# A language-model tower on one core: the prologue between two attention stages becomes 41 small items placed between the parts of attention units

## The reference

```python
h = tok(x)                       # 3 hashed n-gram embeddings per token, concatenated, @ proj_w
h = h + attn(layernorm(h))       # three softmax attentions over the 1024 tokens
h = h + ffn(layernorm(h))        # 32 experts, each takes its 256 best tokens

# attn, per sequence x (1024 x 128):
x_down = conv1d(x, dw, stride=2) + db                     # 512 x 128
a = softmax(q(x) k(x_down)^T * scale);  out_cross = ln(a v(x_down))   # keys: 512
a = softmax(q(x) k(x)^T * scale);       out_dot   = ln(a v(x))        # keys: 1024
a = softmax(qn(x) kn(x)^T / t);         out_cos   = ln(a v(x))        # q, k of unit length
gate = softmax([out_cross, out_dot, out_cos] gw^T + gb)
z = gate0 * out_cross + gate1 * out_dot + gate2 * out_cos
```

## Time and profile before

| | |
|---|---|
| Median of three runs | 1472.56 us |
| The profiled execution | 1471.54 us, its span 1469.3 us |
| PE busy | 1192.1 us (81%) |
| DVE, ACT, POOL busy | 806.1, 641.0, 838.0 us |
| Start of the first unit's maximum | 94.10 us |
| Start of the last unit's maximum | 1079.75 us |
| Start of the second part | 1110.83 us |

### The profile page before, as it was taken

The page is one execution under the profiler, slowest core; times in us unless marked ns, Lnnn a source line. Parts: engine busy times, 40 slices in busy tenths (PEclk is TensorE's granted clock), DMA queues, the critical chain, the costliest instruction groups (busy, mean ns, idle before and its releaser), DMA issues. The chain is left out here.

```text
span 1469.3 us, 25145 instructions
## 1 busy us (share of the span) xinstructions
PE 1192.1 (81%) x7567; PEld 1042.5 (71%) x7567; DVE 806.1 (55%) x2470; ACT 641.0 (44%) x1578; POOL 838.0 (57%) x1223
## 2 busy tenths in 40 slices
PE   3689989998999999799989989998973334666673
PEld 2469968986997898699879969977963323555553
DVE  4256674666667466556656755666775676211110
ACT  0245545554554555356545545654533424211110
POOL 5344764776476467737666764762470002588785
PEclk9889999999999999899999999999985555888786
DMA  2000001001100100100010001001001000344442
GB/s 93 19 22 12 12 15 46 14 5 38 30 12 16 46 12 6 36 26 17 1 56 17 6 26 36 17 1 33 1 16 48 0 0 19 54 83 82 76 76 33
DMA packets 48691, 42.63 MB, mean 29 GB/s; under 512 B 6456, under 2 KB 44088, under 8 KB 48440
## 3 DMA queue, kind: packets, MB, share of 16 engines
q0 software_dynamic: 18432, 22.04, 7.9%
q1 hardware_dynamic: 30136, 19.00, 4.3%
HBM read 27.38 MB, written 13.63 MB: 28 GB/s over the span
## 5 line engine op out<-in xcount | busy, mean ns | idle before, releaser
L957 DVE TENSOR_REDUCE neg_max<-scores 128x1 f32<-128x1024 f32 (+1 forms) x192 | 200.7, 1046 | 222.8 <-PE scores L381 212.7
L573 PEld LDWEIGHTS mixed<-v,pT 128*128 128x128 f32 x2560 | 312.4, 190 | 10.8
L573 PE MATMUL mixed<-v,pT 128*128 128x132 f32 x2560 | 319.5, 276 | 0.0
L1094 ACT ACTIVATE probs<-scores,neg_max 128x1024 f32<-128x1024 f32 (+1 forms) x192 | 187.3, 975 | 288.1 <-DVE neg_max L957 272.9
L1154 POOL DMA_INDIRECT gram<-in_emb,ids_now x192 | 191.0, 995 | 90.1 <-issue 53.9
L1104 ACT ACTIVATE pT<-turned 128x512 f32<-128x512 f32 x320 | 178.6, 595 | 33.5 <-PE turned L537 30.6
L537 PE MATMUL turned<-con,probs 128*128 128x128 f32 x1280 | 173.3, 275 | 3.8 <-ACT w L1075 2.9
L379 PE MATMUL scores<-k_hi,q_hi 128*128 128x512 f32 x320 | 145.3, 454 | 21.0 <-DVE k_lo L752 11.2
L537 PEld LDWEIGHTS turned<-con,probs 128*128 128x128 f32 x1280 | 147.8, 142 | 5.4 <-issue 5.0
L1770 POOL DMA_INDIRECT xg<-token_table,slots x64 | 63.9, 998 | 141.2 <-DVE slots L1655 122.0
L381 PE MATMUL scores<-k_hi,q_lo 128*128 128x512 f32 x320 | 129.7, 405 | 0.0
(11 more groups left out here) (291 smaller groups left out, 2421.1 us busy)
## 6 DMA issues: line engine op xcount, KB each, us to landing
wd<-in_w_down SPq DMA_DIRECT2D x32, 171.0 KB
token_table<-trow SPq DMA_DIRECT2D x8, 640.0 KB, 3.5
out_h<-h SPq DMA_DIRECT2D x8, 512.0 KB, 3.2
gram<-in_emb,ids_now POOLq DMA_INDIRECT x192
wu<-in_w_up SPq DMA_DIRECT2D x8, 170.5 KB, 4.0
w<-in_weights SPq DMA_DIRECT2D x1, 1174.0 KB, 7.2
xg<-token_table,slots POOLq DMA_INDIRECT x64
out_h<-yw,slots POOLq DMA_INDIRECT x64
```

The source lines that it names most:

```text
L573: last = pe.matmul(mixed_of(i), pT[:, i % 2, j * P:(j + 1) * P], vals, start=(j == 0), stop=(j == n - 1))
L957: dve.tensor_reduce(neg_max[:, i % 4:i % 4 + 1], scores[:, (i % 2) * S:(i % 2) * S + n], AX_X, ALU.max, negate=True).then_inc(maxed, 1)
L1094: act.activation(probs[:, i % 2, 0:n], scores[:, (i % 2) * S:(i % 2) * S + n], ACT.Exp, bias=neg_max[:, i % 4:i % 4 + 1], accum_out=exp_su ...
```

## The change

Sequences no longer have a border. The 192 units form one stream, and the pieces of the prologue (and of the embedding and the routing) become **items** with a place in a table, 35 or so per sequence: a line per unit, and in it the items that PE does after the unit's scores, and, behind the bar, those it does before the second half of a mix. One + is the next sequence, two the one after it, a - the one before. For this, k and v have two copies; `turned` and `mixed` are cut to one bank each for the units, and the freed two banks take the items in turn. A unit's transposes and its mix are done in halves of 512 keys, and PE's depth goes from three units to two: step s is score(s), items, turn(s-1), mix(s-2). 27 items of sequence 0 stand ahead of the first unit. No `Fori` is left in the first part, `keep_clock` is gone, the ids are read in place by the gathers (no copy), the tables are stored in halves of four tiles, and the last tiles take the ordinary path. Half of `consts` is now loaded at the start of the second part.

```diff
--- before.py
+++ after.py
...
+
+WHO = dict(gram="av", xT="av", qk_raw="a", down="av", q_d="av", k_d="av", q_cr="av", k_cr="av", q_c="av", k_c="av",
+           v_cr="v", v_dc="v", x2T="a", route="v")
...
+STEADY = ("q_d1 |", "gram6+ | q_cr1", "q_c1 | v_dc0+", "k_d0+ | v_dc1+", "gram7+ | v_dc2+", "qk_raw0+ | v_dc3+",
+          "qk_raw1+ |", "gram8+ |", "x2T1- |", "route1- |", "xT1+ | gram0++", "k_d1+ | qk_raw2+",
+          "down0+ | qk_raw3+", "k_cr0+ | gram1++", "q_d0+ | v_cr0+", "q_cr0+ | v_cr1+", "k_c0+ | gram2++", "k_c1+ | v_dc4+",
+          "q_c0+ |", "gram3++ | v_dc5+", "gram4++ | v_dc6+", "x2T0 | v_dc7+", "gram5++ | route0", "xT0++ |")
...
+
+N = B * UNITS
+TAIL = 12
+ITEMS = [named(word, 0) for word in AHEAD_OF_LOOP.split()]
+PRE = len(ITEMS)
+BANK = [k % 4 for k in range(PRE)]
+PLACED = {}
+for _b in range(B + 1):
+    for _i, _line in enumerate(FIRST if _b == 0 else SECOND if _b == 1 else STEADY):
+        for _where, _part in enumerate(_line.split("|")):
+            _kept = [n for n in (named(word, _b) for word in _part.split()) if 0 <= n[1] < B]
+            PLACED[_b * UNITS + _i, _where] = range(len(ITEMS), len(ITEMS) + len(_kept))
+            ITEMS += _kept
+            BANK += [(len(BANK) + j) % 2 for j in range(len(_kept))]
+AT = {item: k for k, item in enumerate(ITEMS)}
+SLOT_OF = {ITEMS[k]: s for (s, _), ks in PLACED.items() for k in ks}
+A_COUNT, V_COUNT = [0], [0]
...
-        k_hi = [asb(f"k_hi{i}", [P, S if i else SD], F32R) for i in range(BR)]
-        k_lo = [asb(f"k_lo{i}", [P, S if i else SD], F32R) for i in range(BR)]
...
+        k_hi = [[asb(f"k_hi{j}_{i}", [P, S if i else SD], F32R) for i in range(BR)] for j in range(2)]
+        k_lo = [[asb(f"k_lo{j}_{i}", [P, S if i else SD], F32R) for i in range(BR)] for j in range(2)]
...
-        def mixed_of(i):
-
-            return mixed[:, (i % 2) * 512:(i % 2) * 512 + VW]
+        def item_bank(k):
+            return (turned[:, 512:1024], mixed[:, 512:1024], turned[:, 0:512], mixed[:, 0:512])[BANK[k]]
...
-            def keep_clock(b, n):
-
-                pe.wait_ge(exped, b * UNITS)
-                for _ in range(n):
-                    pe.matmul(bank(first("qk_raw")), w_hi[:, 0:P], w_hi[:, 0:512], start=True, stop=True)
...
+            def release(k):
+
+                if k is None:
+                    return
+                name, s, j = ITEMS[k]
+                if "v" in WHO[name] and (name, j) != ("gram", 0):
+                    pe.wait_ge(item_v, V_COUNT[k + 1])
...
+                b, i = divmod(n, UNITS)
+                if half == 0:
+                    pe.wait_ge(exped, n + 1)
+                if n == 0 and half == 0:
+                    release(last_on(2, PRE))
+                else:
+                    pe.wait_ge(pT_ok, b * PARTS + part(i, half) - 1)
+                for j in range(4):
+                    last = pe.transpose(turned[:, j * P:(j + 1) * P], probs[:, n % 2, half * 512 + j * P:half * 512 + (j + 1) * P], ident)
+                last.then_inc(turn_done, 1)
...
+            def mix(n, half):
+                b, i = divmod(n, UNITS)
+                t, br = i // BR, i % BR
+                pe.wait_ge(pT_ok, b * PARTS + part(i, half))
+                if half == 0:
+                    if n == 0:
+                        release(last_on(3, PRE))
                     else:
...
+                        pe.wait_ge(o_ok, n)
+                    if t == 0:
...
+                last_half = half == (0 if br == 0 else 1)
+                for j in range(half * 4, half * 4 + 4):
+                    vals = v0[b % 2][:, j, :] if br == 0 else v12[b % 2][:, j, br - 1, :]
+                    last = pe.matmul(mixed[:, 0:VW], pT[:, n % 2, j * P:(j + 1) * P], vals,
+                                     start=(j == 0), stop=(last_half and j == half * 4 + 3))
+                if last_half:
                     last.then_inc(pv_done, 1)
...
-            prologue(0, None)
-            attention(0, True, None)
-            prologue(1, 0)
-            with pe.Fori(1, B - 1) as b:
-                attention(b, True, b - 1)
-                prologue(b + 1, b)
-            attention(B - 1, False, B - 2)
...
+            pe.wait_ge(ids_ready, 2)
+            for k in range(PRE):
+                item(k)
+            for s in range(N + TAIL):
+                if s < N:
+                    score(s)
+                for k in PLACED.get((s, 0), ()):
+                    item(k)
+                if 0 <= s - 1 < N:
+                    turn(s - 1, 0)
+                if 0 <= s - 2 < N:
+                    mix(s - 2, 0)
+                if 0 <= s - 1 < N and (s - 1) % BR:
+                    turn(s - 1, 1)
+                for k in PLACED.get((s, 1), ()):
+                    item(k)
+                if 0 <= s - 2 < N and (s - 2) % BR:
+                    mix(s - 2, 1)
...
+            for s in range(N + TAIL):
+                if 0 <= s - 3 < N:
+                    output(s - 3)
+                if s % BR == 2 and 0 <= s - 5 < N:
+                    tile_stats((s - 5) // BR)
+                for k in PLACED.get((s - 1, 1), ()):
+                    evict(k)
+                if s < N:
+                    maxima(s)
+                for k in PLACED.get((s, 0), ()):
+                    evict(k)
+                if s % BR == 0 and 0 <= s - 9 < N:
+                    tile_h1_stats((s - 9) // BR)
+                if s % BR == 0 and 0 <= s - 6 < N:
+                    tile_gate_logits((s - 6) // BR)
+                if s % BR == 1 and 0 <= s - 7 < N:
+                    tile_gate((s - 7) // BR)
+                for where in range(2):
+                    for k in PLACED.get((s - 1 - where, where), ()):
+                        if ITEMS[k][0] == "route":
+                            route_probs(*ITEMS[k][1:])
+                for k in items_at(s + 1):
+                    name, seq, j = ITEMS[k]
+                    if name == "xT":
+                        normalise(seq, j)
+                    if name == "k_c" and j == 0:
+                        cos_scale(seq)
...
+            for s in range(N + TAIL):
+                for k in PLACED.get((s - 1, 1), ()):
+                    evict(k)
+                if s % BR == 1 and 0 <= s - 7 < N:
+                    tile_gate_exp((s - 7) // BR)
+                for where in range(2):
+                    for k in PLACED.get((s - 1 - where, where), ()):
+                        if ITEMS[k][0] == "route":
+                            route_exp(*ITEMS[k][1:])
+                if 0 <= s - 1 < N:
+                    keep_turned(s - 1, 0)
+                for k in PLACED.get((s, 0), ()):
+                    evict(k)
+                if s < N:
+                    exponent(s)
+                if 0 <= s - 1 < N and (s - 1) % BR:
+                    keep_turned(s - 1, 1)
+                for k in (*PLACED.get((s - 1, 1), ()), *PLACED.get((s, 0), ())):
+                    if ITEMS[k][0] == "qk_raw":
+                        norm_squares(*ITEMS[k][1:])
...
         @block.gpsimd
         def _(pool):
             def gathers(s, t):
 
-                if t >= 4 or not isinstance(s, int) or s > 0:
-                    pool.wait_ge(gram_turned, s * NT + t - 3)
-                    pool.nop(nofuse=True)
-                pool.tensor_copy(ids_now[:, 3 * t:3 * t + 3],
-                                 ids[:, bass.ds(s, 1), t, :].rearrange("p b g -> p (b g)")).then_inc(staged, 1)
-                pool.wait_ge(staged, s * NT + t + 1)
-                pool.nop(nofuse=True)
+                if t >= 4:
+                    pool.wait_ge(item_full, AT["gram", s, t - 4] + 1)
+                elif s > 0:
+                    pool.wait_ge(item_full, AT["gram", s - 1, t + 4] + 1)
                 for g in range(3):
                     pool.indirect_dma_start(gram[:, t % 4, g, :], None, emb[g],
-                                            bass.IndirectOffsetOnAxis(ap=ids_now[:, 3 * t + g:3 * t + g + 1], axis=0)
+                                            bass.IndirectOffsetOnAxis(ap=ids[:, s, t, g:g + 1], axis=0)
                                             ).then_inc(gathered[t % 4], 16)
...
             token_rstd(0, 1)
-            prologue(0, None)
-            attention(0, True, None)
-            prologue(1, 0)
-            with pool.Fori(1, B - 1) as b:
...
+            cos_norm(0)
+            for s in range(N + TAIL):
+                if s % BR == 2 and 0 <= s - 8 < N:
+                    tile_sum((s - 8) // BR)
+                if s % BR == 2 and 0 <= s - 5 < N:
+                    tile_rstd((s - 5) // BR)
+                if s % BR == 1 and 0 <= s - 10 < N:
+                    tile_x2((s - 10) // BR)
+                for k in items_at(s + 2):
+                    name, seq, j = ITEMS[k]
+                    if name == "xT":
+                        token_rstd(seq, j)
+                    if name == "k_c" and j == 0:
+                        cos_norm(seq)
+                    if name == "gram" and j < NT:
```

(3 more changed lines are left out.)

1010 lines of the change are left out of this document (379 added, 631 removed), and 6 rows, old and new, of tables (FIRST, SECOND).

## The result

The changed kernel takes 1495.3 us (median of 4 runs, 1493.5 to 1497.0), the kernel before, measured beside it, 1472.4: ratio 1.013, 95% interval 1.009 to 1.017. The forecast was 1417. The profiled execution took 1493.5 us with a span of 1491.7.

The account below looks back on a forecast made before the run. PE was taken to set the pace, busy 123.5 of 130.1 us a sequence. 37.7 us saved in the stream, 16 at the start and 1 at the end make 54.7 off 1471.54: 1417 us, range 1390 to 1455.

Parts of the forecast that it names:

- The borders: Between sequences: idle time, low clock and dead matmuls go, so a steady sequence costs PE its work, 118 us.
- Sequence 0 and the start: Ahead of the first score: 16 us saved; in sequence 0, 10 items come back (5 us) and gathers cost 6.
- The clock: PE's clock in the stream: new waits of 0.5 to 1 us are spread out, so nothing was charged.
- The waits that come with depth two: PE's waits in the attention at depth two; with gathers and ACT, 4.5 us of new waits per steady sequence.
- the tightest place: Transposes behind a cos unit's scores, where DVE's maximum is late: a tile without items loses about 0.8 us.
- POOL: POOL's queue, 94 us against 118 per sequence; one or two gathers a sequence expected 1 us late.
- rival C: Gathers late: POOL falls behind in a sequence's second half, five gathers 2 us late each, 1477 us; chance 0.06.
- The last: The last sequence: 77.1 us before, 7 more because few items fill the gaps, 84 us.
- Rival B: Attention: DVE's and ACT's queues hold PE up, each of 64 tiles loses 2.1 us, 1511 us; chance 0.06.
- Rivals A and D: A: items fill every gap, 1380 us, chance 0.20. D: clock falls once a sequence in the stream, 1445 us, 0.08.

Follow-up runs that it names:

- the best version: Changed kernel with DVE's second eviction, normalising and statistics behind the maximum, and gathers issued three units ahead instead of two: 1441.8 us, ratio 0.976.
- the depth test: Kernel before with PE's depth cut to score(i), turn(i-1), mix(i-2) and DVE's output copy one step earlier, ahead of the maximum: 1524.2 us, ratio 1.033.
- DVE mended: Changed kernel with the tile's statistics, DVE's second eviction and normalising moved behind the maximum, gathers still two units ahead: 1478.1 us, ratio 1.001.

## Why the prediction was wrong

The sum, against the profiled execution (1416.8 forecast, 1493.5 measured, 76.7 more):

| | forecast | measured | |
|---|---|---|---|
| first maximum | 78 | 78.2 | |
| sequence 0 | 129 | 149.7 | +20.7 |
| sequence 1 | 122.5 | 135.4 | +12.9 |
| 2 to 5 | 490 | 520.7 | +30.7 |
| 6 | 122.5 | 118.1 | -4.4 |
| last | 84 | 98.4 | +14.4 |
| behind it | 388.6 | 391.2 | +2.6 |
| outside the span | 2.2 | 1.8 | -0.4 |

**Right:** *The borders* and *Sequence 0 and the start* as to the 16 us. PE's work at full clock was forecast at 118 us and is 117.6 in the best version. *The clock* needs no matmuls to hold it in the stream behind sequence 0 (0.97 to 1.00), nor at the borders. The second part took 3.1 us longer, 361.6 instead of 358.5. Sequence 6 came out 4.4 us shorter than forecast because I had given it a full sequence's items, and those of a ninth sequence don't exist.

**Wrong: "The waits that come with depth two".** The step gave 4.5 us for a steady sequence; it is 10.5 of PE idle (129.8 - 119.35). For the tightest place it gave a tile without items 0.8 us; such a tile loses 1.82 (12.00 - 10.18). What failed is that a unit's transposes can start about 2.45 us after its maximum, "and a little for the semaphore":

- The late DVE was right: 4.5 us of its work against 3.7 of PE's were to give 0.8, and the maximum starts about 1.0 late. With the statistics moved behind it 0.95 of the tile go (12.0 - 11.05).
- The 2.45 was wrong: it is 3.06 (1066.53 - 1063.47), against a need of 2.5 us. Between the exponential and the transposes stands ACT's copy of the unit before, 0.60 us, because it frees the bank. With depth three it was never in the way; I had not looked at which copy the transposes wait for.
- "In return for cutting turn and mix in halves nothing is paid" looked at PE's durations and not at the bank. The pair of kernels that differ in this alone shows it: with two banks the halves would have taken the copy out of the way (2.51 us, 10.47 a tile), with one bank it is back (3.09, 11.07).

The 0.85 of the depth test, the halves' -0.55, the bank's 0.60 and the statistics' 0.95 make 1.85, the tile's 1.82. In a steady sequence, where items fill much of this, the units' transposes wait 3.6 us, about what the sum gave to all waits. The rest was not in it: 2.6 for normalised tokens and 2.0 for the output copy in the sequence shown. DVE's order and the gathers' place together bring a steady sequence to 120.3 us.

**Wrong: "POOL"** and rival C. I wrote that one or two gathers a sequence would be 1 us late, and set a price of 1477 with 0.06 on five late ones. By effect this is the larger miss. In the changed kernel as it stands PE's rows show only some 4 us of such waits, since other waits come first; with DVE mended they are 21.8, and one unit more of lead takes 2.5% off. The trace of before could not show this: its gathers stand four tiles ahead. What it did show, POOL's queue full for 47 of 46 us, I turned into a mild wait and not into a rule of when PE would find nothing. (Rival C's 97 us of queue are the 94 of *POOL*.)

**Wrong: sequence 0, 1 and the last.** Of sequence 0's 20.7 us, 16.2 are idle time of PE (22.2 where 6 were counted) and 4.5 are busy time (127.5 where 123 were). 15 us go without gathers: 15 of them, five tiles, follow one another and then nine more, where I had four tiles. The granted clock there is 0.94, so 17 of the 149.7 us are at the lower level; I had charged nothing for it, and it can have cost up to half of that. Sequence 1 has a table of its own, which I did not price: 12.7 us idle and 122.7 busy, and 130.4 us even in the best version. The last: PE's work in it is 11.5 us more than before (87.2 against 75.7), which I had put at nothing. The stretch in the earlier trace rows ends at a maximum and begins in an emptied pipeline; in the stream the end of the sequence before and the last pieces of its own prologue fall into it. Its idle time grew by 9.8 us (1.4 to 11.3) where I had 7.

**Rival B** named 2.1 us a tile (1511) and had 0.06. The result lies nearer to its time than to mine. Of its three parts the 0.8 of DVE and the 0.6 of "one more ACT copy" are in the tile; the 0.7 of evictions is not, since the tile loses 1.82 with hardly an item. Rivals A and D are out. The granted clock was 0.97 in a sequence of the kernel before with and without the matmuls, and 1.00 in a steady sequence of the stream. The Trainium skill (TensorE: Matmul & The Clock Gate, The HAM clock gate) says that the throttled state is the default and that activity releases it. That does not contradict these rows, in which PE is busy nine tenths of the time; it was my step from there to a cost of removing twelve matmuls that they don't bear out.

**Open:** what the gathers do to sequence 0 beyond being late (below), why halves with two banks lengthen the first units of a sequence, and whether ACT's copy, moved ahead of its exponential, would give the 0.6 us back; no kernel tried that.

## What to carry to other kernels

Cutting buffers from two to one to make room for new work is a change of its own: price it as the round trip from writer to reader to writer, not by the writer's durations, and look up what stands ahead of the reader in its own queue. When a pipeline is made shallower, first move everything that may stand behind the reduction that PE waits for, and only then judge the stream: here the orders in DVE's and POOL's queues decided between 1.3% slower and 2.4% faster with the same PE program. And an edit on one in-order queue is read on the others: late gate products made late gathers, early gathers made late powers.

## What the runs showed of the hardware

In the changed kernel signals of matmuls that PE's rows show as done come late at some places. In sequence 0, with 15 gathers in a row from 81.9 on:

```profile
98.38 0.94 POOL L1029 DMA_INDIRECT gram<-in_emb,ids  x1 [0.31 <-issue]
...
103.09 0.29 DVE L831 COPY o<-mixed 128x132 f32<-128x132 f32 x1 [6.89 <-remote]
103.15 0.60 ACT L990 ACTIVATE pT<-turned 128x512 f32<-128x512 f32 x1 [5.10 <-remote]
...
103.89 1.09 PE L564 MATMUL turned<-con,probs 128*128 128x128 f32 x4 [5.26 <-ACT pT L990]
```

The mix and the transposes that the copies wait for ended by 97.3 in PE's rows. "remote" means that no recorded instruction ended when the signal came. Over the whole of the changed kernel such waits make 23.5 us on ACT's copy and 21.5 on DVE's:

```profile
ACT pT L990 <- remote: 23.5, 6, 5.1
DVE o L831 <- remote: 21.5, 4, 7.7
```

In this kernel each of them stands in a row of at least six gathers or up to 3 us behind it: at 103, at 127 to 131, at 214, and then once a sequence, 7 to 9 us after the start of six in a row. With the gathers three units ahead no such row is left behind sequence 0, and no such wait; without the later sequences' gathers there is none in the attention at all. But a row of gathers is not enough: the kernel before with the ids in place has 12 in a row at every border, with 0.3 us between them as here, and no such wait. Whether transfers delay the signal, or the rows of PE lead its real work while it waits for something that the profile does not show, no run here tells.
